# Gated experts kernel on one Trainium2 core: the first product turned round, and the low half of z on GpSimd

## The reference

```python
x = x + tanh(g_xattn) * experts(layernorm(x), ids)      # block 1
x = x + tanh(g_ffn)  * ffn_fp8(layernorm(x), weight)    # block 2

# experts: Wg[e] = Wu[e] = Wd[e] = ctx[e], 512 x 512, e = min(clip(id) // 6250, 3)
a = h @ ctx[e].T ; y = (silu(a) * a) @ ctx[e].T
# ffn_fp8: h and weight quantised to fp8 (e4m3) by their absolute maxima, product, rescaled to bf16
```

## Time and profile before

| what | us |
|---|---|
| median of 3 runs (lowest, highest) | 202.78 (202.16, 204.98) |
| the profiled execution, its own time | 201.43 |
| its span, first to last instruction | 199.7 |
| PE / DVE / ACT / POOL busy in it | 144.3 / 156.3 / 112.7 / 81.8 |

### The profile page before, as it was taken

The page is one execution under the profiler, slowest core; times in us unless marked ns, Lnnn a source line. Parts: engine busy times, 40 slices in busy tenths (PEclk is TensorE's granted clock), DMA queues, the critical chain, the costliest instruction groups (busy, mean ns, idle before and its releaser), DMA issues.

```text
span 199.7 us, 3062 instructions
## 1 busy us (share of the span) xinstructions
PE 144.3 (72%) x723; PEld 69.7 (35%) x727; DVE 156.3 (78%) x351; ACT 112.7 (56%) x166; POOL 81.8 (41%) x117
## 2 busy tenths in 40 slices
PE   0141939998999797999998999999851266566600
PEld 0110424443555343544444445555420223223200
DVE  2876697798758799899989787776686999998820
ACT  2366596887524854688868534233313987666510
POOL 7158787320312344332386673001110023566670
PEclk9999996999999999999999999999997579999985
DMA  0937998200000222111212210000000002132351
GB/s 6 365 113 198 355 408 264 85 2 0 0 3 0 54 56 53 26 39 43 54 26 53 56 26 0 3 0 2 0 5 0 0 0 105 57 153 113 149 208 59
DMA packets 15440, 15.68 MB, mean 79 GB/s; under 512 B 10816, under 2 KB 11328, under 8 KB 15424
## 3 DMA queue, kind: packets, MB, share of 16 engines
q1 hardware_dynamic: 12576, 7.09, 11.8%
q0 software_dynamic: 2560, 8.39, 11.6%
q10 hardware_dynamic: 288, 0.00, 0.1%
HBM read 8.92 MB, written 4.19 MB: 66 GB/s over the span
## 4 chain that ended last, share of the span: by engine, by line
PE 38%; DVE 33%; issue 11%; POOL 7%; ACT 6%; DMA 1%; DVEq 1%; POOLq 0%
PE four_ps L465 10%; PE four_ps L457 10%; PE four_ps L470 9%; DVE w_hi L1044 3%; DVE hT_hi L1052 3%; PE four_ps L498 3%; POOL x L341 3%; PE four_ps L569 2%; DVE bn L880 2%; DVE zT_lo L866 2%; DVE bn L832 2%; DVE x L1056 2%; ACT y L703 2%; DVE z L861 2%; DVE w_lo L824 2%
## 5 line engine op out<-in xcount | busy, mean ns | idle before, releaser
L364 POOL DMA_INDIRECT out<-x,token_of x16 | 19.3, 1208 | 25.4 <-DVE x L1056 22.9
L359 POOL TENSOR_TENSOR rstd<-var,minus_half 128x1 f32<-128x1 f32 x16 | 8.8, 552 | 49.3 <-DVE var L888 49.3
L633 ACT ACTIVATE zT_hi<-four_ps 128x512 f16<-128x512 f32 x19 | 11.3, 595 | 18.9 <-PE four_ps L498 18.9
L457 PE MATMUL four_ps<-w_hi,hT_hi 128*128 x76 | 21.3, 394 | 0.8 <-ACT w_hi L596 0.7
L624 ACT ACTIVATE sg<-four_ps,job_inv_a 128x512 f32<-128x512 f32 x19 | 12.9, 679 | 15.4 <-PE four_ps L470 12.4
L341 POOL DMA_INDIRECT x<-in_x,token_of x16 | 17.4, 1088 | 7.0 <-issue 4.2
L457 PE MATMUL four_ps<-w_hi,zT_hi 128*128 x76 | 19.5, 379 | 0.8 <-ACT zT_hi L633 0.8
L465 PE MATMUL four_ps<-w_lo,hT_hi 128*128 x76 | 19.9, 384 | 0.0
L615 ACT ACTIVATE w<-x,nmr,rstd 128x512 f32<-128x512 f32 x16 | 13.0, 810 | 11.9 <-DVE nmr L894 11.5
L470 PE MATMUL four_ps<-w_hi,zT_lo 128*128 x76 | 19.5, 379 | 0.0
L465 PE MATMUL four_ps<-w_lo,zT_hi 128*128 x76 | 19.5, 379 | 0.0
(11 more groups left out here) (148 smaller groups left out, 293.4 us busy)
## 6 DMA issues: line engine op xcount, KB each, us to landing
w<-in_ctx_t SPq DMA_DIRECT2D x4, 1024.0 KB, 9.4
wf<-in_wf_t SPq DMA_DIRECT2D x1, 512.0 KB, 15.4
x<-in_x,token_of POOLq DMA_INDIRECT x16, 5.9
out<-x,token_of POOLq DMA_INDIRECT x16, 2.9
hT_hi<-h_row SPq DMA_TRANSPOSE x9, 2.3
hT_lo<-h_row SPq DMA_TRANSPOSE x9, 2.3
ids_s<-in_ids SPq DMA_DIRECT2D x1, 8.0 KB, 2.9
g_s<-in_g_x ACTq DMA_DIRECT2D x1, 0.5 KB, 2.7
```

Of the source, the lines that this page charges most:

```text
L364: pool.indirect_dma_start(out, bass.IndirectOffsetOnAxis(ap=token_of[:, i:i + 1], axis=0), block_of(x1, i), None, bounds_check=T - 1).then ...
L457: pe.matmul(ps, lhs_hi(k), w_block(w_hi, expert, k), start=(k == 0), stop=False)
```

## The change

The first product is turned round: the stationary operand is now a 128x128 square of the weights (`w_square`: k-block k, feature block f), the moving operand the 128 tokens of a chunk of hT. Each of the 12 matmuls of 512 columns becomes four of 128 columns, 48 in all, and a comes out as feature by token, which is the form that the second product wants as stationary operand. `transpose_z` and its bank go; the free bank becomes a second buffer for a (a_even, a_odd), and z, zT_hi and zT_lo get two buffers each, chosen by the parity of the job. The high half is now rounded from z in SBUF on ACT (`z_high`), right after z. The low half is made by DVE for jobs 0 to 3 and by POOL from job 4 on (`z_low`), ahead of `rstd_second` in POOL's job. `up(j)` has a new wait for z_done of job j-2, and the waits on the z buffers look one job further back.

```diff
-        a_ps, y_ps, hT_ps, zT_ps = [four_ps[:, n * D:(n + 1) * D] for n in range(4)]
+        a_even, y_ps, hT_ps, a_odd = [four_ps[:, n * D:(n + 1) * D] for n in range(4)]
+        def w_square(t, e, k, f):
+            return t[:, bass.ds(e * (K * D) + k * D + f * P, P)]
+        def a_of(j):
+            return a_odd if j % 2 else a_even
+        def z_part(t, j):
+            return t[:, j % 2 * D:(j % 2 + 1) * D]
...
# POOL
-                pool.wait_ge(zT_done, j)
-                pool.tensor_tensor(z[:, :], az[:, :], sg[:, :], ALU.mult).then_inc(z_done, 1)
+                if j > 1:
+                    pool.wait_ge(zT_lo_done, j - 1)
+                pool.tensor_tensor(z_part(z_two, j), az[:, :], sg[:, :], ALU.mult).then_inc(z_done, 1)
...
+                if E <= j < JOBS:
+                    z_low(j)
                 if E <= j:
                     rstd_second(j - E)
...
+            def z_low(j):
+                pool.wait_ge(zT_hi_done, j + 1)
+                pool.wait_ge(zT_lo_done, j)
+                pool.tensor_tensor(z_part(zT_lo_two, j), z_part(z_two, j), z_part(zT_hi_two, j), ALU.subtract)\
+                    .then_inc(zT_lo_done, 1)
...
# PE: product() goes; up and down have their own loops
             def up(j, tile, expert):
+                first = j < E
                 if j < BY_DMA:
                     pe.wait_ge(hT_hi_done, j + 1)
                 elif j < TILES:
                     pe.wait_ge(hT_landed[j], 32)
+                if j > 1:
+                    pe.wait_ge(z_done, j - 1)
+                def by_hi(k, w, last=False):
+                    for f in range(K):
+                        mm = pe.matmul(a_of(j)[:, f * P:(f + 1) * P], w_square(w, expert, k, f),
+                                       chunk(hT_hi, tile, k), start=(w is w_hi and k == 0 and f == 0), stop=(last and f == K - 1))
+                    return mm
+                def by_lo(last):
+                    if j < BY_DMA:
+                        pe.wait_ge(hT_lo_done, j + 1)
+                    for k in range(K):
+                        for f in range(K):
+                            mm = pe.matmul(a_of(j)[:, f * P:(f + 1) * P], w_square(w_hi, expert, k, f),
+                                           chunk(hT_lo, tile, k), start=False, stop=(last and k == K - 1 and f == K - 1))
+                    return mm
+                for k in range(K):
+                    if first:
+                        pe.wait_ge(w_hi_done, K * j + k + 1)
+                    by_hi(k, w_hi)
+                if first:
+                    by_lo(False)
+                for k in range(K):
+                    if first:
+                        pe.wait_ge(w_lo_done, K * j + k + 1)
+                    mm = by_hi(k, w_lo, first and k == K - 1)
+                if not first:
+                    mm = by_lo(True)
+                mm.then_inc(a_done, 1)
             def down(j, expert):
                 pe.wait_ge(zT_hi_done, j + 1)
                 if not isinstance(j, int) or j > 0:
                     pe.wait_ge(x1_done, j)
+                for t, w in (zT_hi_two, w_hi), (zT_hi_two, w_lo), (zT_lo_two, w_hi):
+                    if t is zT_lo_two:
+                        pe.wait_ge(zT_lo_done, j + 1)
+                    for k in range(K):
+                        mm = pe.matmul(y_ps[:, :], z_part(t, j)[:, k * P:(k + 1) * P], w_block(w, expert, k),
+                                       start=(t is zT_hi_two and w is w_hi and k == 0),
+                                       stop=(t is zT_lo_two and k == K - 1))
+                mm.then_inc(y_done, 1)
-            def transpose_z(j):
-                pe.wait_ge(z_done, j + 1)
-                for k in range(K):
-                    mm = pe.transpose(zT_ps[:, k * P:(k + 1) * P], z[:, k * P:(k + 1) * P], ident[:, :])
-                mm.then_inc(zT_done, 1)
...
# ACT
-            def zT_high(j):
-                act.wait_ge(zT_done, j + 1)
-                if not isinstance(j, int) or j > 0:
-                    act.wait_ge(y_done, j)
-                act.activation(zT_hi[:, :], zT_ps[:, :], ACT.Copy).then_inc(zT_hi_done, 1)
+            def z_high(j):
+                act.wait_ge(z_done, j + 1)
+                if j > 1:
+                    act.wait_ge(y_done, j - 1)
+                act.activation(z_part(zT_hi_two, j), z_part(z_two, j), ACT.Copy).then_inc(zT_hi_done, 1)
...
# DVE: z_of with a_of(j) and z_part; zT_low becomes z_low
-                if not fixed or j < JOBS:
-                    zT_low(j)
+                if j < E:
+                    z_low(j)
```

More of the change, by code:

```diff
@@ L143, in gated_experts_kernel @@
         az = sb("az", [P, D], F32)
-        z = sb("z", [P, D], F32)
-        zT_hi = sb("zT_hi", [P, D], F16)
-        zT_lo = sb("zT_lo", [P, D], F16)
+        z_two = sb("z_two", [P, 2 * D], F32)
+        zT_hi_two = sb("zT_hi_two", [P, 2 * D], F16)
+        zT_lo_two = sb("zT_lo_two", [P, 2 * D], F16)
         bn1 = sb("bn1", [P, 6], F32)
@@ L207, in gated_experts_kernel @@
         hT_hi_done, hT_lo_done = sem("hT_hi_done"), sem("hT_lo_done")
-        a_done, az_done, silu_done, z_done, zT_done = sem("a_done"), sem("az_done"), sem("silu_done"), sem("z_done"), sem("zT_done")
+        a_done, az_done, silu_done, z_done = sem("a_done"), sem("az_done"), sem("silu_done"), sem("z_done")
         zT_hi_done, zT_lo_done, y_done, x1_done = sem("zT_hi_done"), sem("zT_lo_done"), sem("y_done"), sem("x1_done")
@@ L449, in transpose_h @@
                 mm.then_inc(hT_done, 1)
-            def product(ps, lhs_hi, lhs_lo, expert, lo_ready, first=None):
-                for k in range(K):
[L455 to L471, removed]
             def up(j, tile, expert):
+                first = j < E
                 if j < BY_DMA:
@@ L478, in up @@
                     pe.wait_ge(hT_landed[j], 32)
-                def lo_ready():
+                if j > 1:
[6 more added lines that the diff above has]
+                def by_lo(last):
                     if j < BY_DMA:
                         pe.wait_ge(hT_lo_done, j + 1)
-                product(a_ps[:, :], lambda k: chunk(hT_hi, tile, k), lambda k: chunk(hT_lo, tile, k), expert,
-                        lo_ready, j if isinstance(j, int) and j < E else None).then_inc(a_done, 1)
+                    for k in range(K):
[16 more added lines that the diff above has]
+                mm.then_inc(a_done, 1)
             def down(j, expert):
@@ L491, in down @@
                     pe.wait_ge(x1_done, j)
-                product(y_ps[:, :], lambda k: zT_hi[:, k * P:(k + 1) * P], lambda k: zT_lo[:, k * P:(k + 1) * P],
-                        expert, lambda: pe.wait_ge(zT_lo_done, j + 1)).then_inc(y_done, 1)
-            def transpose_z(j):
-                pe.wait_ge(z_done, j + 1)
-                for k in range(K):
-                    mm = pe.transpose(zT_ps[:, k * P:(k + 1) * P], z[:, k * P:(k + 1) * P], ident[:, :])
-                mm.then_inc(zT_done, 1)
+                for t, w in (zT_hi_two, w_hi), (zT_hi_two, w_lo), (zT_lo_two, w_hi):
[6 more added lines that the diff above has]
+                mm.then_inc(y_done, 1)
             def expert_of(j):
@@ L523, in job @@
                     next_tile, next_expert = tile_of(j + 1), expert_of(j + 1)
-                transpose_z(j)
                 if not isinstance(j, int) or j + 1 < JOBS:
@@ L623, in silu @@
                     act.wait_ge(z_done, j)
-                act.activation(sg[:, :], a_ps[:, :], ACT.Silu, scale=job_inv_a[:, bass.ds(j, 1)]).then_inc(silu_done, 1)
+                act.activation(sg[:, :], a_of(j), ACT.Silu, scale=job_inv_a[:, bass.ds(j, 1)]).then_inc(silu_done, 1)
                 if z_on_pool(j):
-                    act.activation(az[:, :], a_ps[:, :], ACT.Copy, scale=job_z_mul[:, bass.ds(j, 1)])\
+                    act.activation(az[:, :], a_of(j), ACT.Copy, scale=job_z_mul[:, bass.ds(j, 1)])\
                         .then_inc(az_done, 1)
-            def zT_high(j):
-                act.wait_ge(zT_done, j + 1)
-                if not isinstance(j, int) or j > 0:
-                    act.wait_ge(y_done, j)
-                act.activation(zT_hi[:, :], zT_ps[:, :], ACT.Copy).then_inc(zT_hi_done, 1)
+            def z_high(j):
[3 more added lines that the diff above has]
+                act.activation(z_part(zT_hi_two, j), z_part(z_two, j), ACT.Copy).then_inc(zT_hi_done, 1)
             def job(j):
@@ L647, in job @@
                 if not fixed or j < JOBS:
-                    zT_high(j)
+                    z_high(j)
                 for i in [2] if j == 0 else first_in(j):
@@ L858, in z_of, with z_low @@
                 dve.wait_ge(silu_done, j + 1)
[L859 to L864, removed]
+                if j > 1:
+                    dve.wait_ge(zT_lo_done, j - 1)
+                dve.scalar_tensor_tensor(out=z_part(z_two, j), in0=a_of(j), scalar=job_z_mul[:, j:j + 1],
+                                         in1=sg[:, :], op0=ALU.mult, op1=ALU.mult).then_inc(z_done, 1)
```

(4 more changed lines are left out.)

## The result

The changed kernel takes 232.35 us, the median of four runs (230.09 to 233.83), beside 202.47 us (201.49 to 204.98) before: a ratio of 1.146, 95% interval 1.134 to 1.158. The forecast was 223 with a range of 207 to 249.

A forecast was written before the change was run, and what follows sets the result against it. TensorE's array, nearly full, bounds block 1 now; afterwards its sequencer would. Profiled 201.4 + 14 x (7.5 - 6.05) + 0.5 - 0.7 = 221.5 us; the median, 1.35 us higher, gives 223, range 207 to 249.

The forecast's parts named there:

- this case: In block 1's jobs, TensorE's sequencer binds at 7.5 us a job: 223 us, own range 216 to 230, chance 0.62.
- rival B: In up's third term, the sequencer makes the w_hi addresses again: 1.54 us more a job, 249 us, chance 0.12.
- First term: four operations that make hT_hi's and a weight's address together (4 x 0.16) and 12 single ones: Sequencer work for up's hT_hi by w_hi products: four operations of 0.16 us and twelve of 0.113 us.
- The step, 7.5 us: Sequencer time of a job in block 1: reads 3 x 0.65, down 1.1, up 4.36, plus 0.1 for longer spacings.
- These cancel ... +0.5: Jobs 0 to 3: later weight products against no transposes ahead of up; up(4)'s end moves from 56.1 to 56.6 us.
- The end ... -0.7: From up(18)'s end to the last down's end: 6.0 us, one read and wait plus two downs, instead of 6.7.
- The low half on GpSimd, worth nothing: Moving z's 0.69 us subtraction from DVE to POOL, 1.16 us there, gains nothing: hidden behind a longer step.
- PE busy for about 70% of block 1: Expected sign in the profile after: TensorE busy about 70% of block 1, clock at 1.00.
- PE still runs without a gap in jobs 14 to 17: Sign in late block 1 jobs that would prove the prediction wrong; up's matmul spacing, 57 ns or more, would tell why.
- Rival C: In block 1, register operations do not bind; PE and VectorE plus waits set some 5.45 us: 193.5 us, chance 0.12.
- Rival D: In up, loads are only partly hidden, 57 to 98 ns a pair, and the sequencer does not bind: 207 us, chance 0.08.
- Rival E: In block 1, starved PE also drops to 1.2 GHz on top of the binding sequencer: 10.3 us a job, 260, chance 0.03.

## Why the prediction was right, and where it was short

Mechanism and sign were right; the time was 9 us too low. Its own range for this case, 216 to 230, also falls short, though the step lies inside its 7.0 to 8.0 us. For the profiled execution the forecast was 221.5 us, and the one whose rows are shown took 232.71: 11.2 us to account for.

- **TensorE's sequencer binds, 36 operations a job, constants not folded, addresses kept (rival B out).** Shown: x304, x304 and x76 in the sequencer's rows, constant addresses that give the whole loss back, more operations and fewer reads that move the step about as counted.
- **A single operation every 0.113 us.** The second term's starts are 0.116 us apart; the size held. What fills the time between two operations that last 32 or 46 ns themselves no run here tells.
- **"First term: four operations that make hT_hi's and a weight's address together (4 x 0.16) and 12 single ones": right in shape, wrong in kind.** All 16 are FUSED_REGOPS; of the first five in the job below two, those with a new chunk of hT_hi, last 84 and 79 ns and the others 46 to 51. On the sequencer the term takes 2.2 us, not 2.0. PE's own spacing of 0.122 hides this, since the first operations run while down's last matmuls do.
- **The step, 7.5 us, measured 7.84: +4.8 us over 14 jobs.** The sequencer's rows of the job of the timeline above (narrow windows):

```profile
L484 PEldq FUSED_REGOPS  x16: 46/46/84, 148.7 to 150.8; - x16
L484 PEldq ALU_OP  x16: 32/32/32, 150.9 to 152.7; - x16
L493 PEldq ALU_OP  x4: 32/32/32, 152.8 to 153.3; - x4
L526 PEldq TENSOR_LOAD <-job_expert_i x1: 300/300/300, 153.4 to 153.4; - x1
L529 PEldq TENSOR_LOAD <-job_tile_i x1: 303/303/303, 155.2 to 155.2; - x1
L484 PEldq FUSED_REGOPS  x4: 46/48/84, 156.4 to 157.0; - x4
```

  The first term takes 2.2 us (148.7 to 150.9), the second 1.9, the third 0.6, the first read with the wait and down 1.8 (153.4 to 155.2), the two other reads 1.2: 7.7 us from one up to the next. The forecast had 2.0, 1.8, 0.45, 1.75 and 1.3, and 0.1 for the new wait, 7.4 us, and 0.1 on top. So the terms are all there and some are mis-sized: the first is too small by 0.2 us, the second and the third by 0.1 to 0.15 each, and "with the 0.1 us that single spacings come out longer" covers only a part. The middle jobs take 7.7 to 7.9 us; their last tenths were not split.
- **"These cancel ... +0.5" for jobs 0 to 4: failed, +3.4.** Two parts. up(4) itself takes 4.73 us to the end of its last record, where it took 2.75; the forecast counted steps from its end and left out up(4)'s own growth, 4.36 - 2.60 = 1.8 by its own figures. And up(4) starts 1.5 us later (53.48 before), because the delay of each early up is handed on in PE's own order. up(2) starts at 37.84 us in both kernels and its last record ends at 41.3 before and 42.7 after; the norms of expert 3 stand behind it and start at 41.57 and 43.24; up(3) starts at 46.01 and 47.13. w_hi of expert 3, for which up(3) waited before, is only 0.8 us later (44.86 and 45.66), and after the change PE no longer waits for it. PE's timeline after, norms of expert 3 and up(4):

```profile
43.24 1.02 PE L451 MATMUL n_ps<-w_lo,ones_bf 128*128 128x512 bf16 x4 [0.56 <-ACT w_lo L613]
...
54.97 1.94 PE L484 MATMUL four_ps<-hT_hi,w_hi 128*128 x16
56.79 1.96 PE L484 MATMUL four_ps<-hT_hi,w_lo 128*128 x16
58.65 1.05 PE L493 MATMUL four_ps<-hT_lo,w_hi 128*128 x16
```

- **"The end ... -0.7": failed, +0.4.** The two last downs now stand one behind the other, and there is one bank for y: down(18) has to wait until add_y(17) has read it. Before, the last transposes and a wait of 0.77 us for the high half stood in that place.

```profile
173.60 1.03 PE L520 MATMUL four_ps<-w_hi,zT_hi_two 128*128 x4 [1.18 <-DVE x L898]
```

- **Block 2, taken as untouched: +2.4**, with a granted clock of 0.76 for 0.84. Not foreseen. The four terms are 4.8 + 2.9 + 1.1 + 2.4 = 11.2 us.
- **The low half on GpSimd, worth nothing: right** (231.01 beside 232.35), and where the sequencer does not bind it seems to cost something, as the text feared: 202.42 with it on GpSimd, 200.14 on VectorE, though the runs overlap (199.79 to 203.29, 199.02 to 201.76).
- **"PE busy for about 70% of block 1": failed.** The column says 98%. It should have been worked out from overlapping records: 0.22 us long, 0.12 apart. The sign "PE still runs without a gap in jobs 14 to 17" comes close to a false alarm for the same reason: 22.54 of 23.30 us are busy in three of these jobs, with one gap of 0.2 to 0.3 us in each. The spacing of the matmuls decides, as the text said.
- **Rival C (193.5): the condition was tried and the price fell too.** With no operation in up it is 202.42; "some 5.45" for the step left out the round of waits in the middle jobs. **Rival D** is out at 0.056 us a pair. **Rival E** is out for the steps at a clock of 1.00, but the lump of reads and the thirteen more operations, at 0.93 and 0.94, show that it was no idle thought.
- **The 62 ns of sequencer a matmul** that the Trainium skill names (same page, section "Step-by-step: what each phase is for", hardware decoding off) are not here: pairs without an operation start every 0.056 us for 48 in a row.

## What to carry to other kernels

Before cutting matmuls into smaller ones with dynamic addresses, count the distinct addresses and ask for the sequencer's rows of the line: here each cost 0.12 to 0.14 us once the sequencer bound, and 36 of them in place of 12 came in for 0.43 us of transposes. A hidden sequencer is a budget (here a microsecond a job) as real as an engine's; keep a register instead of reading it again (0.4 to 0.6 us each once it binds). And when the first of two nearly full engines is relieved, look for a loop of waits through several engines that may hold the step with none of them full.

## What had not been expected of the hardware

- A PE column of 98% can be that of a starved engine: for 128 columns a record lasts 0.22 us while starts can follow at 0.056.
- Idle time of PE can cost twice: 2.60 us of it at a stretch were followed by matmuls at 1.2 GHz (1.88 us for 1.03), and the 14 steps came out 8.5 us longer than with nearly the same work of the sequencer in pieces of some 0.3 us, at a clock of 1.00. It is no sure rule: 2.17 us in a later job of the same run were followed by matmuls at 2.4 GHz, and in another kernel 0.65 us by matmuls at 1.2.
- Block 2 of the same code ran at a granted clock of 0.76 or 0.84 in different kernels, some 2 us apart.
- A starved engine can hide its own clock: with thirteen more operations on the sequencer the steps are 9.4 to 9.7 us whether down's matmuls run at 2.4 or at 1.2 GHz.
